# GELU's second products two tiles behind the first, and output banks that hold two tiles: one Trainium2 core

## What is computed

```python
x = x + 0.5 * L0_ffn(layernorm(x))      # GELU mixture, 128 -> 512 -> 128, 8 experts, top 2
x = x + L0_attn(layernorm(x))           # state space scan
x = x + 0.5 * L0_ffn(layernorm(x))      # GELU mixture
x = x + 0.5 * L1_ffn(layernorm(x))      # SwiGLU mixture, 128 -> 256 -> 128, 8 experts, top 2
x = x + L1_attn(layernorm(x))           # receptance layer
x = x + 0.5 * L1_ffn(layernorm(x))      # SwiGLU mixture

# one expert e of the GELU mixture              # one expert e of the SwiGLU mixture
h = gelu(x @ w1[e] + b1[e])                     h = silu(x @ w1[e].T) * (x @ w3[e].T)
y = h @ w2[e] + b2[e]                           y = h @ w2[e].T
```

## Time and profile before

| | us |
|---|---|
| median of three runs | 1665.01 |
| the profiled execution, its own time | 1676.92 |
| its span, from first to last instruction | 1675.1 |
| PE busy in it | 1122.3 (67%) |
| POOL busy | 768.8 (46%) |
| DVE busy | 805.6 (48%) |
| ACT busy | 551.9 (33%) |

### The profile page before, as it was taken

How to read it: one execution, slowest core, us unless ns; L and a number is a source line. 1 busy time by engine, 2 the same in 40 slices (tenths; PEclk the granted TensorE clock), 3 DMA queues, 4 the chain that set the end, 5 groups by cost and what they waited for, 6 DMA issues and landing times. The chain is left out here.

```text
span 1675.1 us, 28494 instructions
## 1 busy us (share of the span) xinstructions
PE 1122.3 (67%) x6833; PEld 911.2 (54%) x6834; DVE 805.6 (48%) x2947; ACT 551.9 (33%) x1647; POOL 768.8 (46%) x712
## 2 busy tenths in 40 slices
PE   0667788827666787951477776397779764587772
PEld 0567778823356687951466775133343324577771
DVE  1622323257762132425444434459967977254442
ACT  0233456536433454740122323241154121122331
POOL 1445642541055655063656344257724853654434
PEclk9978999968768998985599999599899885789996
DMA  8535567510033455540255665000000000466663
GB/s 242 170 114 177 181 192 227 164 26 0 1 104 131 161 181 172 191 125 12 101 179 193 197 215 175 11 0 1 0 0 0 0 0 18 149 205 208 209 220 111
DMA packets 198074, 199.55 MB, mean 119 GB/s; under 512 B 21493, under 2 KB 139591, under 8 KB 197959
## 3 DMA queue, kind: packets, MB, share of 16 engines
q1 hardware_dynamic: 123138, 136.22, 23.8%
q0 software_dynamic: 16384, 33.59, 7.0%
q10 hardware_dynamic: 58436, 28.41, 5.7%
HBM read 52.27 MB, written 49.02 MB: 60 GB/s over the span
## 5 line engine op out<-in xcount | busy, mean ns | idle before, releaser
L627 ACT ACTIVATE gelu_hid<-gelu_hb,gelu_weights 128x128 f32<-128x128 f32 x736 | 208.8, 375 | 204.9 <-PE gelu_hb L544 147.2
L554 PE MATMUL gelu_ob<-w,gelu_hid 128*128 x1472 | 216.8, 294 | 76.7 <-ACT gelu_hid L627 64.0
L554 PEld LDWEIGHTS gelu_ob<-w,gelu_hid 128*128 128x128 f32 x1472 | 194.3, 206 | 86.6 <-issue 85.8
L857 DVE TENSOR_TENSOR gelu_ys<-gelu_ob,bias 128x128 f32<-128x128 f32 x184 | 53.6, 291 | 367.6 <-PE gelu_ob L554 219.6
L544 PE MATMUL gelu_hb<-gelu_xsT,gelu_weights 128*128 128x128 f32 x1472 | 213.9, 293 | 3.1 <-issue 3.1
L544 PE MATMUL swiglu_hb<-swiglu_xsT,swiglu_weights 128*128 128x128 f32 x1472 | 211.7, 291 | 4.6 <-ACT swiglu_xsT L620 2.6
L544 PEld LDWEIGHTS gelu_hb<-gelu_xsT,gelu_weights 128*128 128x128 f32 x1472 | 198.5, 210 | 3.4 <-issue 3.3
L544 PEld LDWEIGHTS swiglu_hb<-swiglu_xsT,swiglu_weights 128*128 128x128 f32 x1472 | 194.1, 206 | 7.3 <-ACT swiglu_xsT L620 3.4
L1032 POOL DMA_INDIRECT slots_x<-gelu_xn,gelu_index x128 | 124.3, 971 | 137.5 <-DVE gelu_index L817 56.0
L1032 POOL DMA_INDIRECT slots_x<-swiglu_xn,swiglu_index x128 | 124.3, 971 | 132.6 <-DVE swiglu_index L817 59.2
L848 DVE TENSOR_TENSOR swiglu_hid<-swiglu_sil,swiglu_hb 128x256 f32<-128x256 f32 x184 | 76.9, 418 | 212.6 <-ACT swiglu_sil L631 162.7
(11 more groups left out here) (350 smaller groups left out, 1835.3 us busy)
## 6 DMA issues: line engine op xcount, KB each, us to landing
gelu_weights<-w SPq DMA_DIRECT2D x184, 258.0 KB
swiglu_weights<-s SPq DMA_DIRECT2D x184, 256.0 KB
gelu_xs<-slots_x SPq DMA_DIRECT2D x46, 256.0 KB
slots_y<-gelu_ys ACTq DMA_DIRECT2D x92, 128.0 KB
swiglu_xs<-slots_x SPq DMA_DIRECT2D x46, 256.0 KB
slots_y<-swiglu_ys ACTq DMA_DIRECT2D x92, 128.0 KB
slots_x<-zeros SPq DMA_DIRECT2D x2, 1984.0 KB, 12.3
raw_s<-in_L_ffn_w ACTq DMA_DIRECT2D x12, 256.0 KB
```

The costliest lines, as they stand in the source:

```text
L554: last = pe.matmul(o[:, 0:D], hid[:, r, c * P:(c + 1) * P], w2[:, bass.ds(e, 1), c, :].rearrange("p a d -> p (a d)"), start=c == 0, stop=c ...
L627: last = act.activation(hid[:, j % RING, c * P:(c + 1) * P], hb[j][:, c * P:(c + 1) * P], ACT.Gelu, bias=weights[:, j, FF + c:FF + c + 1])
L857: dve.tensor_tensor(y, o, res["bias"][:, bass.ds(e * D, D)], ALU.add).then_inc(y_done, 1)
```

## The change

`LAG` and `RING` become 2 and 4 for both kinds, so that the second products of a GELU tile follow two tiles behind its first ones, with four buffers of `hid` in place of two. For both kinds a bank `ob` now takes the two tiles of a set side by side, and DVE's `output` empties both after the second tile of the set: two additions for GELU, one copy of 128x256 for SwiGLU, which counts `y_done` up by two. PE waits for `y_done` only ahead of the first tile of a set; the value that it waits for is as before, s + 1. The wait of PE for the second part's table moves to the end of the first iteration.

```diff
--- before.py
+++ after.py
@@ -322,7 +322,7 @@
     SET = BODY // 2
     ITERS = NTILES // BODY
 
-    LAG, RING = (1, 2) if gelu else (2, 4)
+    LAG, RING = 2, 4
     BANKS = BODY
     DIGITS = UNROLL * BODY
     assert ITERS * BODY == NTILES and E ** DIGITS <= 2 ** 24 and 2 * SET == BODY and LAG <= SET and LAG + BODY <= DIGITS
@@ -547,11 +547,12 @@
 
             def second_products(s, j, e):
                 pe.wait_ge(hid_ready, s + (1 + BANKS))
-                pe.wait_ge(y_done, s + 1)
-                r, o = j % RING, ob[j % 2]
+                if j % SET == 0:
+                    pe.wait_ge(y_done, s + 1)
+                r, o = j % RING, ob[j // SET % 2][:, j % SET * D:(j % SET + 1) * D]
                 w2 = res["w2" if gelu else "s2"][:, :, :].rearrange("p (e c) d -> p e c d", e=E)
                 for c in range(CH):
-                    last = pe.matmul(o[:, 0:D], hid[:, r, c * P:(c + 1) * P], w2[:, bass.ds(e, 1), c, :].rearrange("p a d -> p (a d)"),
+                    last = pe.matmul(o, hid[:, r, c * P:(c + 1) * P], w2[:, bass.ds(e, 1), c, :].rearrange("p a d -> p (a d)"),
                                      start=c == 0, stop=c == CH - 1)
                 last.then_inc(out_ready, 1)
 
@@ -566,14 +567,14 @@
                     if j == 0:
                         turn_set(i * 2 + 1, 1, i, odd)
                     first_products(s, j, i)
-                    if first and j == LAG + 1:
-                        pe.wait_ge(table_ready, 2)
                     if not (first and j < LAG):
-                        second_products(s - LAG, j - LAG, expert_of(j))
+                        second_products(s - LAG, (j - LAG) % BODY, expert_of(j))
                     if j == 2 and not last:
                         turn_set(i * 2 + 2, 0, i + 1, 1 - odd)
                     for part in beside.get(j, []):
                         part()
+                if first:
+                    pe.wait_ge(table_ready, 2)
                 if last:
                     for d in range(LAG):
                         second_products(NTILES - LAG + d, BODY - LAG + d, expert_of(BODY + d))
@@ -847,16 +848,16 @@
                 dve.wait_ge(out_ready, s + 1)
                 dve.tensor_tensor(hid[:, j % RING, :], sil[:, j, :], hb[j][:, FI:2 * FI], ALU.mult).then_inc(hid_ready, 1)
 
-            def output(s, j, kk, e):
-
-                dve.wait_ge(out_ready, s + 1 + RING)
-                if j % SET == 0:
-                    dve.wait_ge(stored[j // SET], kk * 16 + 16)
-                y, o = ys[j // SET][:, j % SET, :], ob[j % 2][:, 0:D]
-                if gelu:
-                    dve.tensor_tensor(y, o, res["bias"][:, bass.ds(e * D, D)], ALU.add).then_inc(y_done, 1)
-                else:
-                    dve.tensor_copy(y, o).then_inc(y_done, 1)
+            def output(k, half, kk, es):
+
+                dve.wait_ge(out_ready, k * SET + SET + RING)
+                dve.wait_ge(stored[half], kk * 16 + 16)
+                for n in range(SET):
+                    y, o = ys[half][:, n, :], ob[half][:, n * D:(n + 1) * D]
+                    if gelu:
+                        dve.tensor_tensor(y, o, res["bias"][:, bass.ds(es[n] * D, D)], ALU.add).then_inc(y_done, 1)
+                if not gelu:
+                    dve.tensor_copy(ys[half][:, :, :], ob[half][:, 0:SET * D].rearrange("p (j d) -> p j d", j=SET)).then_inc(y_done, SET)
 
             def experts_of(i):
 
@@ -871,13 +872,13 @@
                     s = i * BODY + j
                     if not gelu:
                         multiply(s, j)
-                    if not (first and j < LAG):
-                        output(s - LAG, (j - LAG) % BODY, i if j >= LAG else i - 1, experts[u * BODY + j])
+                    if j % SET == SET - 1 and not (first and j < LAG):
+                        output(i * 2 + j // SET - 1, (j // SET + 1) % 2, i if j >= LAG else i - 1,
+                               experts[u * BODY + j - SET + 1:u * BODY + j + 1])
                     for part in beside.get(j, []):
                         part()
                 if last:
-                    for d in range(LAG):
-                        output(NTILES - LAG + d, BODY - LAG + d, ITERS - 1, experts[BODY + d])
+                    output(NTILES // SET - 1, 1, ITERS - 1, experts[BODY:BODY + SET])
 
             def await_table(p):
                 dve.wait_ge(table_ready, p + 1)
```

## The result

The changed kernel takes 1715.7 us (median of four runs, 1714.1 to 1716.6) against 1664.4 us: 1.028 times as long, 95% interval 1.0205 to 1.0354. Its profiled execution took 1716.5 us with a span of 1714.7, 39.6 us more than that of the kernel before. The forecast of 1674 us, and its range to 1706, were wrong; the time that came lies in the range of rival B.

The account below looks back on a forecast made before the run. PE was taken as the fullest engine but not the sole bound, standing when its signals come late. 1676.9 - 12 + 4 + 3 + 14 = 1685.9, 9 us more; on the median 1665 + 9 = 1674 us, range 1640 to 1706.

Parts of the forecast that it names:

- rival B: SwiGLU's earlier wait isn't absorbed: the 37 us of delay stay or grow towards 74, 1697 to 1734 us; chance 0.14.
- (d): SwiGLU loops: a set's first tile needs an emptying one step later; +14 us, bounds 0 and +74.
- the delay of 37 us before absorption: SwiGLU loops: 49 late signals at 0.75 us each, before taking off 23.1 us of waits for arriving rows.
- (a): GELU loops: more room for ACT, but the y_done wait replaces its wait; -12 us, bounds 0 and -49.
- (c): GELU pairs where nothing is late: up to 0.25 us at a set's first tile; +3 us, at most +19.
- the mean is 2.7 us both times: GELU loops: after a late signal PE stands after 0.9 to 4.5 us, before 1.8 to 3.6; same mean.
- (b): GELU mixtures: a set is stored one tile later, delaying GpSimd's last gathers; 2 us each, +4 us.
- (e): The moved table wait in a mixture's first iteration: nothing; if it showed, a step, 1.8 us.
- The copy of 128x256: DVE's new copy in SwiGLU: taken at 0.42 us, 0.15 us less for DVE per set, so nothing.
- Rival A: GELU breaks free: most of the 48.9 us of waits for ACT go; 1611 us, 1642 with half the gain; chance 0.10.
- The rival's other half: GELU windows: with fewer stops the granted clock of 0.92 rises, at most 25 us more, half of it taken.
- the signs named in the prediction: GELU's ACT waits going without gelu_ys waits in their place (Rival A); SwiGLU loops growing over 20 us each (rival B).

Follow-up runs that it names:

- b_before: The unchanged kernel before, run again for its trace beside the experiments, with signals on time (22 late); 1574.9 us.
- b_after: The changed kernel itself, run again beside the experiments with signals on time; 1594.6 us, 1.0146 of the kernel before (1.0145 once more).
- e1: The changed kernel with y_done started at 3 in place of 2, loosening the wait in both kinds; 1569.3 us, 1.0037 of the kernel before.
- f1: The changed kernel with SwiGLU's wait loosened (y_done started at 3), GELU's left strict; 1591.2 us, 1.0098 of the kernel before.

## Why the prediction was wrong, point by point

**(d) SwiGLU, forecast +14, measured +27** (239.2 to 251.1 and 233.7 to 248.6). The place was right: the first tile of a set waits for an emptying that comes a step later, late signals make it dearer (18.5 to an estimated 37 us), and the waits for rows shrink. Two terms failed. One is missing from the sum, PE's busy time, put at no change without a reason: about half of the growth, 13.7 of 26.7 us, is PE busy for longer, at a lower granted clock (0.95 to 0.90, 0.92 to 0.89). The windows at the head of the first SwiGLU loop, of the kernel before and of the changed one:

```profile
824.00:860.00 36.00, 27.79 (x196) 25.96 (x196) 8.48 (x28) 7.69 (x20) 20.47 (x22) 0.86 0.56 190
```

```profile
838.50:876.00 37.50, 29.89 (x183) 29.00 (x184) 8.70 (x25) 8.55 (x22) 21.50 (x23) 0.73 0.56 189
```

The clock stands at 0.86 there before, and at 0.73 after. Whether the waits bring this about isn't shown; with signals on time the clock was no lower after the change (0.89 and 0.90 against 0.88 and 0.87), and PE was busy for 6.6 and 2.4 us longer all the same (windows 763:968 and 1336:1546 of b_before, 766:981 and 1348:1562 of b_after). That part has another cause than the clock, and it stays open.

The other failed term is the delay of 37 us before absorption. By PE's waits, those for DVE (`swiglu_ys` and `swiglu_hid`) went from 39.1 to 95.6 us, +56; those for rows and `xsT` from 37.6 to 3.4, -34, against 23 assumed. I had counted 49 late signals and nothing for the sets between. But with signals on time, where b_after has 24 late ones in all, the two loops grew by 9.8 and 4.4 us too: the wait is missed by up to 0.3 us in 10 of 46 sets of the first loop, and by 2 us on the mean in eleven where side work stands between; the rows of side work were in the trace. That 34 us were absorbed shows that rival B's reasoning (nothing is absorbed) was wrong as well, although its range held the result.

**(a) GELU's lag, forecast -12, measured +6.1 and +3.6 us in the loops** (with (c) in it). The change of name was right. The step that failed is "the mean is 2.7 us both times", from which I took waits 0.45 us shorter and as many as before: in the windows 48.9 us in 26 waits became 66.4 in 34. The size of one stayed (1.88 and 1.95 us), the number grew. The likely reason, argued and not shown by a run, is that the room isn't a mean: at the first tile of a set it is 0.89 us, and what used to pass under 1.8 us is now felt.

**(b) The store a step later, forecast +4.** Right in kind and too small. The last 24 gathers start 4.4 and 13.2 us later than before (303.0 to 307.4, 712.4 to 725.6), of the latter 3.1 because the loop began later. From the turning of a set to its store it takes 3.5 us longer at the median (15.0 to 18.4), not 2; the rest of the 13.2 is the slower loop. The lag alone costs 3.0 us from turn to store with signals on time, and 0.47% of the time where it has nothing to give. The stretch behind the first GELU loop shrank by 3.4 us, that behind the second grew by 8.1.

**(c) Dense GELU pairs, forecast +3 with a bound of +19.** From the first products of one set to those of the next, the lower decile went from 3.57 and 3.59 to 3.65 and 3.65 us in the two windows: 0.06 to 0.08 us a pair, a third of the 0.25 of the bound. If all 76 paid it, that is an estimated 6 us, of the size of the forecast.

**(e)** Nothing of it was seen. **The copy of 128x256** was taken at 0.42 us, and 0.418 was measured.

**Rival A** had its lag, but not its room; where the wait is loosened (e1) the GELU loops are the shortest of all, 234.0 and 225.5 us, and still the whole is no faster by the medians (1.0037). Part of this is the choice of traces: the profiled execution of e1 was its fastest and that of b_before a slow one, so that they lie 10 us apart in e1's favour, where the medians have 4 us against it. Whether the loosened wait speeds up GELU at all stays open. The rival's other half, a clock that rises with fewer stops, wasn't borne out either: in GELU the granted clock rose from 0.92 and 0.93 to 0.95 and 0.96 while the waits grew in number.

**The chances.** B had 0.14, because one timeline showed absorption. It did absorb; what was not asked is how often a set pays with nothing late at all. By the signs named in the prediction neither rival came: GELU's waits took the name `gelu_ys`, and the SwiGLU loops grew by 12 and 15 us, under the 20 of rival B. That the time fell into B's range is luck of that range: (a), (b) and (d) each came out dearer than forecast.

## What to carry to other kernels

When buffers are merged in pairs and the wait for them is kept, work out anew which use of the buffer it protects: here one credit more in the semaphore, `sem_inc(y_done, 3)`, took back 1.1 of 1.45%, and in SwiGLU left the pairing without a cost that could be measured (0.9988). A wait that moves by one place in a queue passes everything that stands there, so list the side work between the old place and the new, and not only the rare events that first drew attention; and try a control, since here moving the side work helped the kernel before as well. Room that a lag is to give counts only if every wait of the step has it, and is paid for by a later store, which costs wherever another engine's chain starts from it.

## What the runs showed of the hardware

- TensorE's signals were late in some groups of runs and not in others, the same kernel taking 1664 to 1672 us or 1565 to 1571. Groups recorded under the same chip number gave both (1568 us in one, 1672 in another), at the same mean granted clock (0.857 and 0.849 in the traces of before). With late signals 347 to 405 of 1357 came over 0.8 us late, without 17 to 32. What decides it is open; nothing in the kernels does. Whether the late signals are what makes these groups 6% slower, or another sign of the same thing, isn't shown.
- An operation of VectorE with two operands in SBUF was held while GpSimd added in SBUF: 10.0 us in place of 0.22 (L777 in f1), till the additions of 9.22 us ended, while additions of VectorE with one operand in PSUM took 0.57 us for two beside the same work. The Trainium skill (page SBUF — State Buffer, section "SBUF: two separate sides") says that the two engines share a port pair that one of them holds for a whole instruction, and that VectorE needs it for two SBUF inputs beside a GpSimd operation that reads SBUF. The trace agrees on which operations are held and which are not; but the hold lasted over four instructions of GpSimd in a row (1.3, 3.4, 3.4 and 1.3 us), not one.

The additions that weren't held:

```profile
586.85 8.05 POOL L1039 TENSOR_TENSOR x<-x,post_b 128x1536 f32<-128x1536 f32 x3
...
589.63 0.57 DVE L858 TENSOR_TENSOR gelu_ys<-gelu_ob,bias 128x128 f32<-128x128 f32 x2 [4.39 <-PE gelu_ob L555]
```
